# Routing of a mixture of experts: rows gathered through a slot table instead of rows scattered through DRAM

## The reference, cut to what matters

```
x = x + gnn(layernorm(x), edges, ...)           # h + update of the nodes
t = layernorm(x)                                # tokens, 6250 x 256
probs = softmax(t @ router_w.T); rw, re = top_k(probs, 2); rw /= rw.sum()
y = t + sum over the two experts e of rw_e * (gelu(t @ w1[e] + b1[e]) @ w2[e] + b2[e])
x = x + y
```

## Time and profile before

| | us |
|---|---|
| median of 3 runs | 2843.23 (2842.95 to 2843.74) |
| the profiled execution | 2843.46 |
| its span, first to last instruction | 2841.7 |
| PE busy | 2395.3 (84%) |
| DVE busy | 1999.0 (70%) |
| ACT busy | 1685.5 (59%) |
| POOL busy | 1282.3 (45%) |
| mean granted clock of TensorE | 0.916 |

### The profile page before, as it was taken

How to read it: one execution, slowest core, us unless ns; L and a number is a source line. 1 busy time by engine, 2 the same in 40 slices (tenths; PEclk the granted TensorE clock), 3 DMA queues, 4 the chain that set the end, 5 groups by cost and what they waited for, 6 DMA issues and landing times. The chain is left out here.

```text
span 2841.7 us, 61657 instructions
## 1 busy us (share of the span) xinstructions
PE 2395.3 (84%) x15142; PEld 2059.0 (72%) x15143; DVE 1999.0 (70%) x6013; ACT 1685.5 (59%) x5927; POOL 1282.3 (45%) x1335
## 2 busy tenths in 40 slices
PE   4388888769999999999999999999999890039990
PEld 4277777647888888888888888888888790038880
DVE  8978888547777777777777877777777664323335
ACT  2766666537777777777777777777776560013330
POOL 2045555625555555555555555555552113644440
PEclk7699989879999999999999999999999995569995
DMA  6010000133233333223332233332243772223338
GB/s 141 3 29 25 27 25 26 33 102 94 86 89 90 89 89 90 87 89 90 90 89 87 88 90 89 90 89 86 88 89 49 214 227 75 93 100 120 123 102 271
DMA packets 151899, 259.47 MB, mean 91 GB/s; under 512 B 32176, under 2 KB 96889, under 8 KB 151448
## 3 DMA queue, kind: packets, MB, share of 16 engines
q0 software_dynamic: 57392, 140.00, 17.8%
q1 hardware_dynamic: 87392, 111.96, 13.0%
q10 hardware_dynamic: 7025, 6.40, 0.7%
HBM read 195.46 MB, written 62.80 MB: 91 GB/s over the span
## 5 line engine op out<-in xcount | busy, mean ns | idle before, releaser
L1033 POOL DMA_INDIRECT work<-dst_half,stage_i x848 | 814.1, 960 | 780.2 <-PE ps L1241 581.0
L1224 PE MATMUL ps<-W2c,work 128*128 128x256 f32 x3392 | 802.3, 379 | 0.0
L1224 PEld LDWEIGHTS ps<-W2c,work 128*128 128x128 f32 x3392 | 612.0, 190 | 70.7
L1059 DVE TENSOR_TENSOR agg<-agg,ps 125x256 f32 x848 | 354.7, 418 | 254.1 <-PE ps L1241 246.4
L1165 ACT ACTIVATE work<-ps 128x512 f32<-128x512 f32 x424 | 252.1, 595 | 353.5 <-PE ps L1241 349.2
L1241 PE MATMUL ps<-work 128*125 128x256 f32 x1696 | 435.2, 379 | 1.3 <-ACT work L1186 1.3
L1180 ACT ACTIVATE work<-work 128x256 f32<-128x256 f32 x848 | 341.6, 404 | 53.5 <-DVE work L1086 49.1
L1215 PE MATMUL ps<-ablk,work 128*128 x2544 | 352.3, 275 | 20.5 <-DVE work L1107 9.8
L1138 DVE SCALAR_TENSOR_TENSOR work<-ps,work,b2c 128x256 f32<-128x256 f32 x848 | 368.7, 477 | 0.0
L513 POOL DMA_INDIRECT edge_records<-stage,work x208 | 229.1, 1101 | 279.8 <-PE ps L927 185.7
L1172 ACT ACTIVATE work<-work 128x256 f32<-128x256 f32 x848 | 340.8, 406 | 3.3 <-issue 3.1
(11 more groups left out here) (277 smaller groups left out, 3313.1 us busy)
## 6 DMA issues: line engine op xcount, KB each, us to landing
work<-tile_sources SPq DMA_DIRECT2D x106, 250.0 KB
work<-routed_tokens SPq DMA_DIRECT2D x53, 257.0 KB
work<-dst_half,stage_i POOLq DMA_INDIRECT x848
routed_tokens<-work SPq DMA_DIRECT2D x26, 514.0 KB
work<-expert_rows SPq DMA_DIRECT2D x25, 320.0 KB, 5.3
update_node_half<-work SPq DMA_DIRECT2D x25, 250.0 KB, 2.2
work<-update_node_half SPq DMA_DIRECT2D x25, 250.0 KB
work<-expert_rows SPq DMA_DIRECT2D x25, 180.0 KB, 6.0
```

The lines of the kernel that those rows point to most:

```text
L1033: pool.indirect_dma_start(bg[:, r, u, :], None, dstd, bass.IndirectOffsetOnAxis(ap=stage_i[:, c:c + 1], axis=0)).then_inc(gath[r], 16)
L1059: v.tensor_tensor(d, d, ps[0:NB, (7, 0)[a.mod(2)], u * D:(u + 1) * D], ALU.add).then_inc(agg_add, 1)
L1224: last = t_.matmul(ps[:, 5 + s, u * D:(u + 1) * D], sT[:, a.mod(RT), u, k], W2c[:, k], start=(k == 0), stop=(k == KC - 1))
```

## The change

- The update stores the normalized tokens once, in token order, to a new DRAM tensor `tokens`: SP issues two stores for each pair of blocks, seven steps behind (`US`), and waits for `tb_ready`. `tb` gets four buffers. The empty rows and their buffer are gone. SP issues the loads of the experts' weights after this loop, as before.
- The top-2 block gets a slot table. The position of each of the 100 pairs of block and choice (`RK`) is split into its row of 128 and its tile. For each of ten batches DVE makes one-hot rows (1280 columns in one operation) and ten times one-hot tiles multiplied by the token's number (106 columns). TensorE sums the 100 products of 128 x 106 into PSUM; the result, clamped and halved, is `slot_token`, the token of each slot. Empty slots read token 0. ACT adds the tokens to `agg` meanwhile, 50 operations.
- Routing is gone. In the experts' stage POOL gathers each tile of 128 rows from `tokens` by `slot_token`, 106 gathers, up to four pairs ahead of TensorE (`LEAD`). The results are stored by SP in slot order, one plain DMA for each pair.
- The combination gathers from `expert_rows` by the slots of the tokens (`xposi`): four indirect DMAs on POOL for each pair of blocks, 100 in all, written without a loop, where SP had two plain ones.

The diff, cut to its core (declarations of semaphores and buffers are left out):

```diff
-XW = D + 1
-XD = 8
-assert XT + 16 <= P
+RK = K2 * BK
+assert XT + 16 <= P and XT % 2 == 0 and RK % SB == 0
...
-        xsd = nc.dram_tensor("routed_tokens", (XT * P + 8 * (P - NB), XW), f32).ap()
-        yd = nc.dram_tensor("expert_rows", (K2 * N + XD * P, D), f32).ap()
+        tokd = nc.dram_tensor("tokens", (N, D), f32).ap()
+        yd = nc.dram_tensor("expert_rows", (XT * P, D), f32).ap()
...
@@ update of the nodes, sync @@
-                        empty_slots(m)
-                pipeline(sp, NP2, UA, RP, step, peel=2)
-                for g in range(NP2 * XD // 2, XT, XD // 2):
-                    d, o = min(XD // 2, XT - g), g % XD
-                    sp.dma_start(xsv[:, g:g + d, :], padrow[:, o:o + d]).then_inc(xpads_out, 16)
+                    a = m - US
+                    if a.within(NP2):
+                        r = a.mod(RTB)
+                        sp.wait_ge(tb_ready, a.of(1, 1))
+                        rows = tokd[bass.ds(a.of(2 * NB), 2 * NB), :].rearrange("(u p) f -> p u f", p=NB)
+                        for p in PARTS:
+                            sp.dma_start(rows[p], tb[r][p]).then_inc(tb_out[r], 16)
+                pipeline(sp, NP2, US, RP, step, peel=2)
...
-                sp.wait_ge(xpads_out, 16 * -(-XT // (XD // 2)))
+                for r in range(RTB):
+                    sp.wait_ge(tb_out[r], 32 * len(range(r, NP2, RTB)))
...
@@ update of the nodes, scalar @@
-                        wait(act, tb_tr, a.of(1, -1))
+                        wait(act, tb_tr, a.of(1, 1 - RTB))
+                        wait(act, tb_out[a.mod(RTB)], a.per(RTB, 32, 0))
...
@@ top-2, vector @@
+                v.tensor_scalar(xscale[n_], mv3[n_, :, 1], 1.0, None, ALU.add).then_inc(coef_ready, 1)
...
-                link(v.tensor_copy(xposi[n_], xposf[n_].rearrange("p k t -> p t k")))
+                link(v.memset(xposi[P // 4 * 3:P], 0))
+                link(v.tensor_copy(xposi[n_].rearrange("p (t k) -> p t k", k=K2), xposf[n_].rearrange("p k t -> p t k")))
+                link(v.tensor_copy(posi[n_], xposf[n_].rearrange("p k t -> p (k t)")))
+                link(v.tensor_scalar(hiix[n_], posi[n_], P - 1, None, ALU.bitwise_and))
+                link(v.tensor_scalar(loix[n_], posi[n_], 7, None, ALU.arith_shift_right))
+                link(v.tensor_copy(hix[n_], hiix[n_]))
+                link(v.tensor_copy(lox[n_], loix[n_]))
+                for s in range(RK // SB):
+                    r = s % RN
+                    wait(dve, xinv, s - RN + 1)
+                    v.tensor_tensor(hi2[n_, r], hix[n_, s * SB:(s + 1) * SB].unsqueeze(2).to_broadcast([NB, SB, P]),
+                                    iota_f[n_, :].unsqueeze(1).to_broadcast([NB, SB, P]), ALU.is_equal).then_inc(xop_ready, 1)
+                    for c in range(s * SB, (s + 1) * SB):
+                        v.tensor_scalar(lov2[n_, r, c - s * SB], iota_f[n_, 0:XT], lox[n_, c:c + 1], sval[n_, c:c + 1],
+                                        ALU.is_equal, ALU.mult).then_inc(xop_ready, 1)
+                dve.wait_ge(xinv, RK // SB)
+                link(v.tensor_scalar(rank, ps[:, 6, 0:XT], 1.0, -1.0, ALU.max, ALU.add))
+                link(v.tensor_scalar(slot_token, rank, 1, None, ALU.arith_shift_right))
...
@@ top-2, scalar and tensor @@
+                act.wait_ge(coef_ready, 1)
+                for t in range(BK):
+                    nc.scalar.activation(agg[n_, t, :], agg[n_, t, :], ACT.Identity, bias=mv3[n_, t, 0:1],
+                                         scale=xscale[n_, t:t + 1]).then_inc(xt_added, 1)
...
+                for s in range(RK // SB):
+                    pe.wait_ge(xop_ready, (s + 1) * (SB + 1))
+                    for c in range(SB):
+                        last = t_.matmul(ps[:, 6, 0:XT], hi2[n_, s % RN, c], lov2[n_, s % RN, c],
+                                         start=(s + c == 0), stop=((s + 1) * SB + c == RK + SB - 1))
+                    last.then_inc(xinv, 1)
...
@@ experts: the routing of POOL and DVE is gone; sync and gpsimd now @@
+                def step(m):
+                    y = m - L2
+                    if y.within(XP):
+                        r = y.mod(RY)
+                        sp.wait_ge(yb_ready, y.of(1, 1))
+                        sp.dma_start(yd[bass.ds(y.of(2 * P), 2 * P), :].rearrange("(u p) n -> p u n", p=P), yb[:, r]).then_inc(y_out[r], 16)
+                pipeline(sp, XP, L2, RX, step)
+                for r in range(RY):
+                    sp.wait_ge(y_out[r], 16 * len(range(r, XP, RY)))
...
+                def gather(m):
+                    wait(pool, xs_tr, m - LEAD + 1)
+                    for u in range(2):
+                        pool.indirect_dma_start(xs[:, m % RX, u], None, tokd,
+                                                bass.IndirectOffsetOnAxis(ap=slot_token[:, 2 * m + u:2 * m + u + 1],
+                                                                          axis=0)).then_inc(xs_in[m % RX], 16)
+                for m in range(XP):
+                    gather(m)
...
@@ combination: in place of SP's loads @@
+            @block.gpsimd
+            def _(pool):
+                for m in range(NP2):
+                    wait(pool, acc_add, 4 * (m - RF + 1))
+                    for u in range(2):
+                        for k in range(K2):
+                            c = (2 * m + u) * K2 + k
+                            pool.indirect_dma_start(yin[:, m % RF, u, k], None, yd,
+                                                    bass.IndirectOffsetOnAxis(ap=xposi[:, c:c + 1], axis=0)).then_inc(yin_in[m % RF], 16)
```

More of the change, by code:

```diff
@@ L1300, in gnn_moe_kernel @@
         aggcp = two(u=2)
-        tb = two(u=2)
+        RTB = 4
+        tb = [cut(2 * D, "p (u n) -> p u n", u=2) for _ in range(RTB)]
         tT = two("p (k n) -> p k n", KC * 2 * NB, k=KC)
-        padrow = cut(XD * XW, "p (d w) -> p d w", d=XD)
         raw3 = cut(12, "p (u s) -> p u s", u=2)
@@ L1307, in gnn_moe_kernel @@
         half3 = cut(2)
-        padrow_set = sem("padrow_set")
-        xpads_out = sem("routed_pads_out")
+        tb_out = [sem(f"tokens_out{r}") for r in range(RTB)]
         uw_in = sem("uw_in")
@@ L1553, in step @@
                         wait(pe, tT_ready, a.of(1, 0))
[L1554 removed]
+                        transposes(3, tb[a.mod(RTB)], tb_tr)
                 update(pe, step)
@@ L1732, in _ @@
             def _(sp):
[L1733 to L1745, removed]
-                nc.gpsimd.iota(tslot[tail].rearrange("p r k -> p (r k)"), pattern=[[P - NB, RS * K2]],
-                               base=XT * P + tail.start - NB, channel_multiplier=1).then_inc(ts_spare, 1)
-                def route(m):
-                    r = m.mod(RS)
-                    wait_apart(pool, ts_ready, m.of(1, 1), passed_pool)
-                    for k in range(K2):
-                        pool.indirect_dma_start(xsd, bass.IndirectOffsetOnAxis(ap=tslot[:, r, k:k + 1], axis=0),
-                                                ts[:, r, k], None).then_inc(ts_out[r], 16)
-                pipeline(pool, BK, 0, RS, route)
                 def step(m):
@@ L1771, in _ @@
                 v = nc.vector
-                def route(m):
-                    r = m.mod(RS)
-                    wait(dve, ts_out[r], m.per(RS, 16 * K2, 0))
-                    wait(dve, xt_added, m.of(1, 1 - RS))
-                    t = bass.ds(m.of(), 1)
-                    v.tensor_scalar(ts[n_, r, :, 0:D], agg[n_, t, :].to_broadcast([NB, K2, D]),
-                                    mv3[n_, t, 1], mv3[n_, t, 0], ALU.mult, ALU.add).then_inc(ts_parts, 1)
-                    v.tensor_copy(tsr[n_, r, :, D], home[n_, t, :].rearrange("p t k -> p (t k)"))
-                    v.tensor_copy(tslot[n_, r], xposi[n_, t, :].rearrange("p t k -> p (t k)")).then_inc(ts_ready, 1)
-                    dve.wait_ge(ts_parts, m.of(1, 1))
-                    v.tensor_tensor(agg[n_, t, :].rearrange("p t f -> p (t f)"), agg[n_, t, :].rearrange("p t f -> p (t f)"),
-                                    ts[n_, r, 0, 0:D], ALU.add).then_inc(xt_added, 1)
-                dve.wait_ge(ts_spare, 2)
-                for t in range(BK):
-                    route(Step(0, RS, t))
                 regs = [v.alloc_register(f"expert_of_tile{j}") for j in range(2 * (RX + L2))]
@@ L1813, in step @@
                         dve.wait_ge(y_ps, a.of(1, 1))
-                        wait(dve, y_out[r], a.per(RY, 32, 0))
+                        wait(dve, y_out[r], a.per(RY, 16, 0))
                         for u in range(2):
@@ L1906, in gnn_moe_kernel, with _ @@
         with nc.Block() as block:
-            @block.sync
-            def _(sp):
-                def step(m):
-                    r = m.mod(RF)
-                    wait(sp, acc_add, m.of(4, 4 - 4 * RF))
-                    rows = yd[bass.ds(m.of(2 * NB * K2), 2 * NB * K2), :]
-                    byrow = rows.rearrange("(u p k) n -> p u k n", p=NB, k=K2)
-                    for p in PARTS:
```

(6 more changed lines are left out.)

59 lines of the change are left out of this document (26 added, 33 removed).

## The result

The changed kernel took 2835.09 us (median of 12 runs, 2827.97 to 2838.24) against 2844.14 for the kernel before, run beside it: ratio 0.997 [0.9962, 0.9978]. It is faster, by about 9 us where 20 were forecast, and inside the forecast range. Of all the executions in this document one was in a slow state (5345.76 us, one of the four of r9_dve_line), and no reading rests on it.

What follows compares the result with a forecast made beforehand. TensorE paced the experts, transfers the combination, and routing kept TensorE waiting. Terms 12.4 + 38.8 - 142.0 + 0.6 - 10.5 + 80.8 = -19.9 us from 2843.46 gave 2824, range 2808 to 2844.

Steps and rivals of the forecast that it cites:

- term 5: Combination: 100 POOL gathers in straight-line code, with 5.9 us of stall, take 141.9 us instead of 61.1: +80.8.
- term 3: Routing: removed before the first transposes, two gathers being enough, -142.0 us; second tile late in the experts' ramp, +0.6.
- Term 1: End of the update: expert weights queue behind the last token store and arrive later, +12.4 us.
- term 2: Top-2 chain: the new slot table, ten batches paced by DVE, delays POOL's opening of the next block, +38.8 us.
- clock rival: Slot table: TensorE at the low clock sets the pace instead of DVE, +6.6 us, so 2831; chance 0.12.
- Term 4: Experts to combination: POOL's drain is covered, so the gap is 3.1 us instead of 13.6, -10.5.
- contention rival: Combination: gathers and DVE's additions hold each other up, 16 to 48 us, so 2840 to 2872; chance 0.16.

Runs made afterwards that it cites:

- r9_dve_line: Changed kernel with DVE's part of the combination written out with constants instead of a register loop; 2794.55 us, 0.9945 of the kernel before.
- r6_again: Changed kernel, unaltered, run again on a chip where the kernel before takes 2841 to 2844 us; 2834.61 us, 0.9974 of the kernel before.
- r1_again: Changed kernel, unaltered, run again on a chip where the kernel before takes 2808 to 2809 us; 2793.18 us, 0.9946 of the kernel before.
- r11_w_line: Changed kernel with expert weights issued in the update's closing steps and DVE's combination written out without registers; 2814.85 us, 0.991 of the kernel before.

## Why the prediction was wrong in size

The step that failed is the stall of term 5, put at the 5.9 us for which POOL had stood still in routing; POOL waited 12.2 us for buffers that DVE had not emptied, because DVE's queue was slow. A late start of DVE in the ramp of term 3, of the same or another cause, cost 3.2 us (+3.8 for +0.6), and the sum had nothing for it. The two are 9.5 of the 10.5 us between -19.9 and -9.4. Why DVE's queue is slow on A stays open.

- **Term 1** (weights behind the last tokens) was +14.0 for +12.4 and **term 2** (table of slots) +37.8 for +38.8, so that two small errors nearly cancel. The clock rival (0.12) did not come. At the low clock (0.50 from 2390 to 2394, TensorE busy 3.85 of 4.00 us) the first two batches took 6.56 us together; from 2394 on the clock was 0.99 to 1.00, each later batch took 2.48, and DVE paced.
- **Term 3** was right for the stage removed, on A. Its ramp was not: "the second is about 0.6 late in the ramp: +0.6" counted POOL's 2.53 us per pair and nothing for DVE. It was +3.8, and +6.2 in r6_again; r1_again, without the late starts, has +0.6 against the profiles of before.
- **Term 4** was right (-10.4).
- **Term 5** is the mis-sized one, +87.1 for +80.8, by its own parts: between gathers I had 99 x 1.26 = 124.7 and 5.9 of stall; the chip took 1.246 apart (123.3), 3.2 of stretch and 12.2 of stall. The end I had at 11.3 from the last gather's start, and it took 9.5. So -1.4 + 3.2 + 6.3 - 1.8 = +6.3. But for the stall the parts cancel, which is luck.
- The stall stood in the trace of before, and I added it as it was. DVE's waits in the same stretch of before, which I had not put into the sum, are larger:

```profile
DVE agg L1784 <- remote: 34.0, 12, 4.6
```

  Routing hid most of it behind POOL's own pace. I carried over what POOL stood still and not what held DVE up; in the combination POOL depends on DVE for every buffer. Without any stall my sum is 136.0, and r1_again measured 136.1. That they agree so closely is luck as well: between the gathers it took 2.0 more than my 124.7, and at the end 1.9 less than my 11.3.
- **The bounds** of the terms sum to 2809 at the lower end, and I wrote 2808; nothing rests on it.
- **The contention rival** named the pair of engines and the wrong mechanism: additions stretched gathers by 3 us in all, not 16 to 48. By the Trainium skill (SBUF — State Buffer, Who interferes with whom) the later of the two waits out the other, and gathers of up to 1.28 us agree; the slow queue instructions are something else, since ACT has them too.
- **On B** the change gave 15 us. The combination is 5.8 shorter than forecast there, and yet the gain is 5 short. That the routing of before is shorter on B as well is argued, not shown: before's median less 1.8 and less 2320.6, the mean start of the last tokens on B, is 486 us, against 498 in the mean of the profiles on A. With 12 us less to remove and 5.8 less to pay, -19.9 becomes -14.

## What stays open

What resource is short, why on A only, whether the rate of indirect transfers, POOL's straight-line code or something else brings it on, whether the late starts and the long instructions are one thing, and what the experts' stage with 212 transfers would take on B.

## What to carry to other kernels

A stage paced by indirect transfers back to back has a second price: other engines' queues may run late, here on the chips of kind A alone, so measure on both kinds before believing 0.5%. Look for it in the minimum, median and maximum of the queue's own instructions, and in "remote" and "issue" waits of engines that aren't the bottleneck. Weights should be issued before the last dependent store, not behind it: that was worth 13 us on B and 15 on A, where the whole change gave 15 and 6 to 9; with it and DVE's combination written out the kernel takes 2814.85, 0.991 [0.9893, 0.9926] of before.

## What the runs showed of the hardware

Unexpected was that small instructions of DVE's or ACT's queue have common ceilings in slow stretches: FUSED_REGOPS of DVE's additions and of ACT's stores (medians 47 to 99 ns) and ACT's store-issuing instruction (346) came to 1396 to 1398 ns, ACT's MOVE (29) to 1387, and DVE's ALU_OP (40) to 702 to 721, about half of that. In r11_w_line, where DVE has no such instructions, ACT's queue had the long ones. POOL's drain was hidden between experts and combination, as forecast. An indirect transfer of 128 rows took POOL 1.25 to 1.28 us, as a gather (945 ns in the experts of the changed kernel) or as a store (958 in those of before), each with 0.30 of issue.
